# Perceiver block on one Trainium2 core: softmax row sums of the cross attention summed into the output banks, reciprocal over 128 partitions, and TensorE's batches written out

## The reference, cut to what matters

```python
def _L0_xattn_ref(x, context, mask, Wq, Wkv, Wo, bo):   # H, DH = 16, 64; x 8x128x512, context 8x2048x512
    q = x @ Wq
    k, v = jnp.split(context @ Wkv, 2, axis=-1)
    q, k, v = heads(q), heads(k), heads(v)
    sim = jnp.einsum('bhid,bhjd->bhij', q, k) * DH ** -0.5
    sim = jnp.where(mask[:, None, None, :], sim, -jnp.finfo(sim.dtype).max)
    attn = jax.nn.softmax(jnp.clip(sim, -5.0, 5.0), axis=-1)
    out = jnp.einsum('bhij,bhjd->bhid', attn, v)
    ...
x = x + _L0_xattn_ref(_layernorm(x), ctx, mask, ...)
x = x + _L0_attn_ref(_layernorm(x), ...)
x = x + _L0_ffn_ref(_layernorm(x), ...)
```

## Time and profile before

| what | value |
|---|---|
| median of 3 runs | 3756.53 us (3754.54 to 3761.86) |
| the profiled execution | 3767.23 us |
| its span, first to last instruction | 3765.4 us |
| PE busy | 3469.4 us, 92% |
| DVE busy | 1943.5 us, 52% |
| POOL busy | 1607.0 us, 43% |
| ACT busy | 1463.9 us, 39% |
| first scores of the cross attention | 109.20 us |
| next stage's first DMA after it | 2214.38 us |

### The profile page before, as it was taken

How to read it: one execution, slowest core, us unless ns; L and a number is a source line. 1 busy time by engine, 2 the same in 40 slices (tenths; PEclk the granted TensorE clock), 3 DMA queues, 4 the chain that set the end, 5 groups by cost and what they waited for, 6 DMA issues and landing times. The chain is left out here.

```text
span 3765.4 us, 52065 instructions
## 1 busy us (share of the span) xinstructions
PE 3469.4 (92%) x18834; PEld 2932.0 (78%) x18834; DVE 1943.5 (52%) x3079; ACT 1463.9 (39%) x2676; POOL 1607.0 (43%) x1068
## 2 busy tenths in 40 slices
PE   5999999999999999999999968989896866999998
PEld 4888888888888888888888857777675554787886
DVE  4455555555555555555555556656656365221115
ACT  3455554554554554545545431434533152110000
POOL 3455554455555544545554541314412251433340
PEclk9999999999999999999999988999998988999999
DMA  5111111111110101111110032000001201211111
GB/s 196 62 43 38 39 32 44 34 43 43 41 36 32 43 35 44 43 35 33 41 43 34 15 113 62 25 25 1 2 1 57 62 1 37 62 45 45 45 45 39
DMA packets 103885, 161.30 MB, mean 43 GB/s; under 512 B 10192, under 2 KB 70736, under 8 KB 94928
## 3 DMA queue, kind: packets, MB, share of 16 engines
q1 hardware_dynamic: 103632, 158.02, 12.9%
HBM read 139.12 MB, written 18.87 MB: 42 GB/s over the span
## 5 line engine op out<-in xcount | busy, mean ns | idle before, releaser
L424 POOL TENSOR_TENSOR e_hl<-e,e_hl 128x512 fp32r<-128x512 f32 x512 | 663.3, 1296 | 1048.2 <-ACT e L489 1048.2
L485 ACT ACTIVATE e_hl<-sc 128x512 fp32r<-128x512 f32 x512 | 324.0, 633 | 800.0 <-DVE sc L553 799.0
L589 PE MATMUL ps_p<-c_hi,wkv_lo 128*128 128x512 f32 x1024 | 410.3, 401 | 31.7 <-DVE rec L529 19.5
L511 DVE TENSOR_TENSOR k_lo<-ps_p,k_hi 128x512 fp32r<-128x512 f32 x256 | 177.2, 692 | 446.9 <-ACT k_hi L449 446.0
L589 PE MATMUL ps_p<-c_lo,wkv_hi 128*128 128x512 f32 x1024 | 404.5, 395 | 0.0
L589 PE MATMUL ps_p<-wkv_lo,c_hi 128*128 128x512 f32 x1024 | 402.0, 393 | 0.0
L589 PE MATMUL ps_p<-wkv_hi,c_lo 128*128 128x512 f32 x1024 | 401.9, 392 | 0.0
L589 PE MATMUL ps_p<-c_hi,wkv_hi 128*128 128x512 f32 x1024 | 401.8, 392 | 0.0
L589 PE MATMUL ps_p<-wkv_hi,c_hi 128*128 128x512 f32 x1024 | 398.7, 389 | 0.0
L511 DVE TENSOR_TENSOR v_hl<-ps_p,v_hl 128x512 fp32r<-128x512 f32 x256 | 176.6, 690 | 409.5 <-ACT v_hl L449 409.5
L553 DVE TENSOR_SCALAR sc<-ps_s,topi 128x512 f32<-128x512 f32 x512 | 379.7, 742 | 10.0 <-PE ps_s L639 9.9
(11 more groups left out here) (350 smaller groups left out, 7173.5 us busy)
## 6 DMA issues: line engine op xcount, KB each, us to landing
raw<-in_ctx_t SPq DMA_DIRECT2D x64, 1024.0 KB, 4.9
dense_raw<-in_L_ffn_W_experts SPq DMA_DIRECT2D x32, 512.0 KB, 3.5
raw<-in_L_xattn_Wkv SPq DMA_DIRECT2D x4, 1024.0 KB, 4.9
q_hi_scratch<-qa_qh SPq DMA_DIRECT2D x16, 256.0 KB, 2.5
q_lo_scratch<-qa_ql SPq DMA_DIRECT2D x16, 256.0 KB, 3.3
q_hi<-q_hi_scratch SPq DMA_DIRECT2D x32, 128.0 KB, 3.8
q_lo<-q_lo_scratch SPq DMA_DIRECT2D x32, 128.0 KB, 3.8
o_t_scratch<-o_sb SPq DMA_DIRECT2D x32, 128.0 KB, 1.8
```

The lines of the kernel that those rows point to most:

```text
L424: g.tensor_tensor(E2[:, s % 2, :, 1, :], E[:, s % 2].rearrange("p (j q) -> p j q", j=GRP), E2[:, s % 2, :, 0, :].bitcast(F32), ALU.subtrac ...
L485: a.activation(E2[:, s % 2, :, 0, :], sc, ACT.Exp, scale=DH ** -0.5).then_inc(exp_hi, 1)
L511: v.tensor_tensor(kv_slice(False, kind, n), ps_view(u, kind), kv_slice(True, kind, n).bitcast(F32), ALU.subtract).then_inc(p_free, 1)
L589: mm = t.matmul(ps_p[:, par % 2, :], lhs, rhs, start=m == 0, stop=m == 3 * KC - 1)
```

## The change

Three things are altered, all in stage_cross.

The total is moved out of ps_p. It now goes into the first 256 columns of the first of the group's own two ps_o banks, after the output was read out of them: four matmuls of 256 columns in place of two of 512. There are two matrices of ones, each with ones in 64 of its columns and zeros in the other 64, so that the sums of the even heads land in partitions 0 to 63 and those of the odd heads in 64 to 127. total now waits for o_read besides es_lo, and no longer for p_free. The ring of ps_p holds projections alone (unit_at).

The group's output is packed the same way. ScalarE copies in four instructions over 64x256 in place of two over 64x512, VectorE adds U in two in place of one, and GpSimd's add, the reciprocal and the multiplication are one instruction each over 128x256. The multiplication and the store go from L+5 to L+6. The first values of the next group in these banks wait for the reciprocal (rec_done) and not for o_read.

TensorE's eight batches are written out; the other engines keep the loop over batches 1 to 6. The lines that are left out of the diff below rename arguments or set the two matrices of ones.

```diff
@@ -275,12 +275,12 @@
-        T1 = sb("t1", [DH, GRP, P])
-        T2 = sb("t2", [DH, GRP, P])
-        U = sb("u", [DH, GRP, P])
-        REC = sb("rec", [DH, GRP, P])
...
+        T1 = sb("t1", [P, 2, P])
+        T2 = sb("t2", [P, 2, P])
+        U = sb("u", [P, 2, P])
+        REC = sb("rec", [P, 2, P])
@@ -298,6 +298,7 @@
         scored, clipped, exp_hi, expd, e_lo = sem("scored"), sem("clipped"), sem("exp_hi"), sem("expd"), sem("e_lo_done")
         summed, es_hi, es_lo = sem("summed"), sem("es_hi_done"), sem("es_lo_done")
         pv_done, o_copied, o_read, u_done, o_done, o_out = (sem(n) for n in ("pv_done", "o_copied", "o_read", "u_done", "o_done", "o_out"))
+        totalled, rec_done = sem("totalled"), sem("rec_done")
@@ -323,13 +324,9 @@
-        def ring(s, first, last, which):
-
-            before = min(s, SL - KT) if last else s
-            before += sum(len(after(x, 4)) for x in range(s)) + (which == "sum" and has_kv(s, last))
-            return NA + before - (0 if first and s <= 3 else 1)
-
-        NU = SL + 4
+        def unit_at(i, s):
+
+            return i * SL + NA + s
@@ -343,15 +340,7 @@
-        TAIL = range(SL, SL + 6)
+        TAIL = range(SL, SL + 7)
@@ -375,7 +364,7 @@
             queries(0, 1)
 
             def store(i, hf, GL):
-                sp.wait_ge(o_done, 2 * (4 * i + 2 * hf + GL + 1))
+                sp.wait_ge(o_done, 4 * i + 2 * hf + GL + 1)
@@ -393,17 +382,19 @@
                     if s == SL // 2 and not last:
                         sp.wait_ge(scored, S)
                         queries(i + 1, 0)
-                    for n in after(s, 5):
+                    for n in after(s, 6):
                         if n >= 0 or not first:
                             store(i - (n < 0), n % 4 // 2, n % 2)
@@ -414,7 +405,7 @@
                         g.tensor_tensor(ES_lo[:], ES[:, n % 2], ES_hi[:].bitcast(F32), ALU.subtract).then_inc(es_lo, 1)
                 for n in after(s % SL, 4):
                     if n >= 0 or not first:
-                        g.wait_ge(o_read, 4 * i + n + 1)
+                        g.wait_ge(o_read, 2 * (4 * i + n + 1))
                         g.tensor_tensor(U[:], U[:], T2[:], ALU.add).then_inc(u_done, 1)
 
             for u, (kind, n) in enumerate(AHEAD):
-                evac_hi(0, u, kind, n)
-
-            def group_steps(i, s, first, tail=False):
+                evac_hi(u, u, kind, n)
+
+            def group_steps(i, s, first):
                 s %= SL
                 for n in after(s, 2):
                     if n >= 0 or not first:
                         L = ENDS[n % 4][0] - SL * (n < 0)
                         a.wait_ge(summed, i * SL + L + 1)
                         if not first or n > 0:
-                            base, u = sum_ring(i, n - 1, False, tail)
-                            a.wait_ge(proj_done, base + u + 1)
+                            a.wait_ge(totalled, 4 * i + n)
                         a.copy(ES_hi[:], ES[:, n % 2]).then_inc(es_hi, 1)
                 for n in after(s, 3):
                     if n >= 0 or not first:
@@ -467,17 +457,16 @@
                         a.wait_ge(pv_done, i * SL + L + 1)
                         if not first or n > 0:
                             a.wait_ge(u_done, 4 * i + n)
-                        o4 = ps_o[:, 2 * (n % 2):2 * (n % 2) + 2, :].rearrange("p b (j e q) -> p (b j) e q", j=2, e=2)
-                        a.copy(T2[:], o4[DH:P, :, 0, :]).then_inc(o_copied, 1)
-                        a.copy(T1[:], o4[0:DH, :, 1, :]).then_inc(o_copied, 1)
+                        o4 = ps_o[:, 2 * (n % 2):2 * (n % 2) + 2, :].rearrange("p b (j e q) -> p b j e q", j=2, e=2)
+                        for hh in range(2):
+                            a.copy(T1[hh * DH:(hh + 1) * DH], o4[0:DH, :, hh, 1, :]).then_inc(o_copied, 1)
+                            a.copy(T2[hh * DH:(hh + 1) * DH], o4[DH:P, :, hh, 0, :]).then_inc(o_copied, 1)
 
         @block.vector
-            def group_steps(i, s, first, tail=False):
+            def group_steps(i, s, first):
                 s %= SL
                 for n in after(s, 3):
                     if n >= 0 or not first:
-                        v.wait_ge(o_copied, 2 * (4 * i + n + 1))
+                        v.wait_ge(o_copied, 4 * (4 * i + n + 1))
                         if not first or n > 0:
-                            v.wait_ge(o_done, 2 * (4 * i + n))
-                        o4 = ps_o[0:DH, 2 * (n % 2):2 * (n % 2) + 2, :].rearrange("p b (j e q) -> p (b j) e q", j=2, e=2)
-                        v.tensor_tensor(U[:], o4[:, :, 0, :], T1[:], ALU.add).then_inc(o_read, 1)
+                            v.wait_ge(o_done, 4 * i + n)
+                        o4 = ps_o[0:DH, 2 * (n % 2):2 * (n % 2) + 2, :].rearrange("p b (j e q) -> p b j e q", j=2, e=2)
+                        for hh in range(2):
+                            v.tensor_tensor(U[hh * DH:(hh + 1) * DH], o4[:, :, hh, 0, :], T1[hh * DH:(hh + 1) * DH], ALU.add
+                                            ).then_inc(o_read, 1)
                 for n in after(s, 5):
                     if n >= 0 or not first:
-                        base, u = sum_ring(i, n, False, tail)
-                        v.wait_ge(proj_done, base + u + 1)
-                        v.reciprocal(REC[:].rearrange("p j q -> p (j q)"), ps_p[0:DH, u % 2, :]).then_inc(p_free, 1)
-                        v.wait_ge(p_free, base + u + 1)
+                        v.wait_ge(totalled, 4 * i + n + 1)
+                        v.reciprocal(flat(REC[:]), ps_o[:, 2 * (n % 2), 0:2 * P]).then_inc(rec_done, 1)
+                for n in after(s, 6):
+                    if n >= 0 or not first:
+                        v.wait_ge(rec_done, 4 * i + n + 1)
                         v.wait_ge(u_done, 4 * i + n + 1)
                         if not first or n > 0:
                             v.wait_ge(o_out, 16 * (4 * i + n))
-                        for hh in range(2):
-                            v.tensor_tensor(O_sb[hh * DH:(hh + 1) * DH], U[:, hh::2, :], REC[:, hh::2, :], ALU.mult).then_inc(o_done, 1)
+                        v.tensor_tensor(O_sb[:], U[:], REC[:], ALU.mult).then_inc(o_done, 1)
         @block.tensor
@@ -595,7 +584,7 @@
                 hf, blk, GL, kt = place(s)
                 t.wait_ge(e_lo, S + 1)
                 if blk == 0 and kt == 0 and (hf or not first):
-                    t.wait_ge(o_read, 4 * i + 2 * hf + GL - 1)
+                    t.wait_ge(rec_done, 4 * i + 2 * hf + GL - 1)
                 for j in range(GRP):
                     mm = t.matmul(ps_o[:, 2 * GL + j // 2, (j % 2) * 256:(j % 2 + 1) * 256], V2[:, kt, GRP * GL + j, :],
                                   E2[:, s % 2, j].rearrange("p e q -> p (e q)"),
@@ -603,13 +592,17 @@
                                   skip_group_check=True)
                 mm.then_inc(pv_done, 1)
 
-            def total(i, n, last, tail):
-
-                base, u = sum_ring(i, n, last, tail)
+            def total(i, n):
+
                 t.wait_ge(es_lo, 4 * i + n + 1)
-                t.wait_ge(p_free, base + u - 1)
-                t.matmul(ps_p[:, u % 2, :], ONES[:], ES_lo[:], start=True, stop=False)
-                t.matmul(ps_p[:, u % 2, :], ONES[:], ES_hi[:], start=False, stop=True).then_inc(proj_done, 1)
+                t.wait_ge(o_read, 2 * (4 * i + n + 1))
+                m = 0
+                for part in (ES_lo, ES_hi):
+                    for hh in range(2):
+                        mm = t.matmul(ps_o[:, 2 * (n % 2), 0:2 * P], ONES[:, hh, :], part[:].rearrange("p (c h q) -> p c h q", c=2, h=2)[:, :, hh, :],
+                                      start=m == 0, stop=m == 3)
+                        m += 1
+                mm.then_inc(totalled, 1)
 
@@ -623,12 +616,8 @@
                     S = i * SL + s
                     hf, blk, GL, kt = place(s)
-                    if first and s < 2:
-                        t.wait_ge(p_free, 2 * (s + 1))
-                    elif s < 2:
-                        t.wait_ge(p_free, (i - 1) * NU + ring(SL + s - 2, False, False, "kv") + 1)
-                    elif has_kv(s - 2, last):
-                        t.wait_ge(p_free, i * NU + ring(s - 2, first, last, "kv") + 1)
+                    if s < 2 or has_kv(s - 2, last):
+                        t.wait_ge(p_free, unit_at(i, s - 2) + 1)
@@ -646,17 +635,17 @@
-                        u = ring(s, first, last, "kv")
-                        t.wait_ge(p_free, i * NU + u - 1)
-                        project(kind, n, of, cb, u)
+                        t.wait_ge(p_free, unit_at(i, s) - 1)
+                        project(kind, n, of, cb, unit_at(i, s))
                     for n in after(s, 4):
                         if n >= 0 or not first:
-                            total(i, n, last, False)
-
-            over_batches(t, body)
+                            total(i, n)
+
+            for i in range(B):
+                body(i, i == 0, i == B - 1)
```

(46 more changed lines are left out.)

## The result

The changed kernel takes 3690.66 us (median of 4 runs, 3688.79 to 3699.55) against 3759.2 us for the kernel before (4 runs, 3754.54 to 3764.04): ratio 0.9822, 95% interval 0.9801 to 0.9844. The forecast was 3691 us, with a range of 3682 to 3710. In a later comparison the same kernel took 3696.21 us (3690.27 to 3700.41) against 3757.64: ratio 0.9829 (0.9813 to 0.9846).

A forecast was written before the change was run, and what follows sets the result against it. TensorE, busy 92% of the span, was taken as the bound. Group waits (-49.4), jumps (-17.5), lateness at jumps (+1.5), extra matmuls (+0.6) and the stage's end (-0.6) gave 3756.5 - 65.4 = 3691 us, range 3682 to 3710.

The forecast's parts named there:

- The count of lost time by stretches: Cross attention batches: 254.0 us without waits; each loses 6.6 us without TensorE's jump, 10.1 us with one.
- rival C: TensorE's straight instruction stream starves, three stalls a batch costing 82 us, time 3773 us; chance 0.04.
- The walk through the handover: VectorE's steps around a group's end: 1.2 us slack at slot 32's scores, 0.4 at looped boundaries, no mid-batch wait.
- rival A: Only part comes back, as VectorE's and ScalarE's lateness is real work: 3702, up to 3717 us; A or B 0.20.
- Reshaped steps: Group's end: reciprocal 1.7 us, copy about 380 ns, addition near 420 ns; four total matmuls add 0.6 us in all.
- Rival B: VectorE's reciprocal goes by elements, staying 3.34 us: +9 us, 3700 us; A or B together 0.20.
- Sum: All terms: -49.4 - 17.5 + 1.5 + 0.6 - 0.6 = -65.4 us, from the median of 3756.5 us.
- The split: Cross attention gains: 49.4 us from group losses at 8 mid-batch events and 7 boundaries, 17.5 us from TensorE's five jumps.
- Rival D: Stall ahead of a batch's first scores is the other engines' jumps, not TensorE's: 3709 us; chance 0.06.
- The reason named for the gain: At group ends, taking the total out of the ps_p ring removes both ring waits, together 49.4 us.
- The added wait: The total now needs VectorE's U, forecast done 1.4 us ahead of it in mid-batch.
- End of the stage: Chain from the last group's copies to the next stage: about -0.6 us, between -1.5 and +1.

The follow-up runs named there:

- ring-out kernel: Kernel before with TensorE's batches written out and the total moved to the output banks as two 512-column matmuls, nothing packed: 3706.71 us, ratio 0.9865.
- the changed kernel looped: Changed kernel with only TensorE's batches put back into a loop: 3720.58 us, ratio 0.9895 to the kernel before; stage 2074.9 us.

## Why the prediction was right, and where it was not

- *The count of lost time by stretches* held: 254.0 us a batch was forecast and 254.08 measured, seven times. Every wait that was listed went. TensorE's straight stream shows no stall in any stretch, so rival C is out.
- *The walk through the handover* held to a tenth: v_lo ends at 996.0 and the scores that need it start 1.3 us later (1.2 forecast). At slot 1 behind the other engines' jumps the same difference, the start of the scores less the end of the read of their unit, was 0.24 to 0.58 us in five batches (0.4 forecast). The 1.5 us that I charged there did not come, and neither did rival A.
- *Reshaped steps*: the reciprocal 1.75 us (1.7), a copy 368 ns (380), an addition 418 ns (420), the slot with a total 4.42 us. Four matmuls in place of two cost 0.11 us a batch (254.08 against 253.97 us in the ring-out kernel), 0.9 us in all (0.6). Rival B is out.
- *Sum*: the stage gave 66.0 us, 65.4 were forecast. That the first median agrees to 0.4 us is partly luck: it is 68.5 us below its companions, the second comparison 61.4, and in the two profiles most of the difference is the self attention's clock. Two small slips change nothing: the floor of the sum is 3688.7 and not 3688, and the terms given for the end of the stage add up to -0.5 and not -0.6.
- *The split* was wrong, though its sum held. I put 49.4 us on the ring and packing and 17.5 on TensorE's jumps, as if they added. In the stage, TensorE straight alone gives 8.9 us, ring and packing alone (the changed kernel looped) 42.9, and both 66.0: 14 us belong to neither. (The medians say so more strongly: 3.2 and 38.1 of 68.5 us, or of 61.4 in the second comparison.) The step that failed is "TensorE's jump itself costs 3.5 us", taken from 264.1 - 260.6. That difference is the price of the jumps of all engines at a boundary: with none of them the stage of the kernel before is 18.3 us shorter (17.5 forecast), and ring and packing then bring 47.2 (49.4 forecast). TensorE's jump alone is worth 1.8 us there, since 9.4 us of the others' jumps then come out from under it; in the changed kernel, where theirs are covered by slack, it is worth 4.6, 23.1 us for the five in place of 18.3. The 9.4 and these 4.8 us are the 14. The 4.8 agree with group waits that had lain under the stalls: rec and v_hl at projections take 26.4 us in the kernel before and, with all its engines straight, 30.9:

```profile
PE ps_p L587 <- DVE rec L527: 22.2, 30, 1.3
PE ps_p L587 <- DVE v_hl L509: 8.7, 21, 0.9
```

The half clock is not the difference: it followed all five jumps in the kernel before and four of five in the changed kernel looped.
- *Rival D* got 0.06. For this kernel it was wrong (with TensorE looped again 23 us return), but its mechanism is real: it is why straight code alone gave half.
- *The reason named for the gain* was the ring's order more than the reciprocal's length. Shown: 50.8 of 57.1 us without any packing, if with the multiplications a slot later. But packing alone would have given 28.0, which the text did not say.
- *The added wait.* I had U done 1.4 us ahead of the total and gave the scores behind it 1.2 us. The changed kernel has 1.54 and 1.29 in batch 3, so the verdict (nothing waits) and the order of the two margins were right. With the copies doubled the list of waits names the total, because it stands first; by the rows both places are then at their limit. What I had not seen is that lateness carries over to the next group.
- *End of the stage*: -0.6 us was forecast; from the values of slot 18 of batch 7 to the next stage it took 184.81 us before and 181.61 now, 3.2 less, of which 3.1 are that batch's middle. So nothing. Its start, put at nothing, got 0.4 us longer.

## What to carry to other kernels

Where one engine sets the time, compare equal stretches of its stream with a clean stretch: the difference is all there is to win, whatever the list of waits says. A small unit that shares a ring of two buffers with a large one takes away a whole step of slack for both, and a free bank elsewhere can be worth more than a faster instruction. When two causes of a wait lie over one another, neither is worth its full price alone: take them out together, and test by putting back one at a time. A difference between boundaries with and without a loop's jump is the price of the jumps of all engines there, not of the one whose stall shows.

## What the runs showed of the hardware

In the changed kernel looped, a taken jump of TensorE in a loop of about 1400 matmuls costs 2.75 to 3.3 us of issue, and the half clock (512-column matmuls 0.63 us against 0.39) followed it in four of five cases; in the kernel before it followed in five of five. ScalarE and VectorE lose 1.1 to 1.2 us at theirs. VectorE's reciprocal takes 3340 ns over 64x512 and 1746 ns over 128x256. An unchanged stage with many short waits of TensorE differed by 9 us between two executions of the same code, at a granted clock of 0.96 and 0.98. What starts one or the other was not found: right ahead of the half-clock step at 2408.29 us of the kernel before, TensorE had been idle for 1.73 and 0.81 us, and so it had ahead of a step of the changed kernel (at 2600.25 us) that ran at the full clock.
